# Edge attributes of a graph network kept in full precision, in bands of 32 partitions

## The chip, the cores and the metric

The kernel runs on one core of a Trainium2 chip as one launch. The time is that of one execution on the device in microseconds (us), and lower is better. The engines are TensorE (PE; its weight loads are listed as PEld), VectorE (DVE), ScalarE (ACT), GpSimd (POOL) and SyncE (SP). Each engine takes its instructions in the order in which they are written, and they meet over semaphores.

## The reference

A stack of graph networks and feed-forward layers over 1875 nodes of 256 features. Its first stage, the one that the change bears on, is a network of four layers over 31875 edges, which are ordered by their destination. Each edge has 32 attributes.

```python
def _gine(x, src, dst, edge_attr, W1, b1, W2, b2, eW, eb, eps):
    e = edge_attr @ eW + eb      # 31875 x 32 by 32 x 256
    m = jax.nn.relu(x[src] + e)
    agg = jax.ops.segment_sum(m, dst, num_segments=N)
    h = (1.0 + eps) * x + agg
    return jax.nn.relu(h @ W1 + b1) @ W2 + b2

h = _gine(x, src, dst, edge_attr, W1[0], b1[0], W2[0], b2[0], eW[0], eb[0], eps[0])
for k in range(1, 4):
    y = jax.nn.relu(_layernorm(h, gamma[k], beta[k]))
    h = h + _gine(y, src, dst, edge_attr, W1[k], b1[k], W2[k], b2[k], eW[k], eb[k], eps[k])
```

Behind it come a feed-forward layer with a capacity, an attention over edges with eight relations (it uses the same sorted edges), mixtures of experts and two graph convolutions. The change leaves them as they are.

## The kernel before, in words

**Order of the program.** `sort_edges` brings the edges into 264 chunks of 128 (`EC`), so that each chunk's edges go to nodes of one tile of 128 (15 tiles). It ends in `unpack_rows`. Then `pair_edges` builds tables for a later stage, mostly with GpSimd, and `gine_stack` runs the four layers: a layer norm, `gine_edges` (the edge loop) and `gine_mlp` (two products by 256 x 256 weights). All stages run one behind the other.

**Unpacking.** The 264 chunks arrive as rows of 36 words in 11 groups of `K` = 24 chunks. SyncE issues the loads of 9 chunks of each group, ScalarE those of 7, GpSimd those of 8 (`lanes`, L360). When a group is there, VectorE writes its 32 attributes four times side by side in bf16 (L440 and `split3`, L322 to L332): the high part, the middle part (what is left behind the high part), the low part, and the high part again. TensorE turns each chunk, 128 edges by 4 x 32 parts, with a bf16 transpose (L408, 264 of them, four to a PSUM bank), and ScalarE (22) and VectorE (44) copy the banks to `g.attrs_t` (L368), one block of 128 partitions by 128 edges for each chunk. VectorE takes out sources, destinations, types and weights too: for ten groups at once behind the tenth group's split, and for the last group behind its own (L417 to L427). `g.attrs_t` is a bf16 view of `g.edge_space`, 128 x 16896 words, whose memory the later attention uses again.

**Edge loop.** `gine_edges` runs once in each layer, over 264 chunks:

- GpSimd fetches for each chunk the 128 rows of the sources, 256 words each, from the table in DRAM with one indirect DMA (L833). The ring `got` has `RING` = 24 places. Before it issues chunk c it waits until the sum product of chunk c - 24 is done.
- TensorE makes the edge product of chunk c, two bf16 products over 128 rows that add up in one PSUM bank (L883, L884): the four parts of the attributes by parts of the weights, so that the sum stands for the full-precision product. Before it, it waits until VectorE has added chunk c - 4 (`summed`), which frees the bank.
- VectorE adds the edge product to the gathered rows (L922) once both are there. It also makes the one-hot matrices of the destinations, four chunks at a time (L844).
- ScalarE applies the relu in place (L901).
- TensorE makes the sum product of chunk c - 3 right behind the edge product of chunk c: gathered rows by one-hot matrix, two halves of 128 x 128 in full precision (L893). They wait for the relu (`msg_ready`) and for the bank that VectorE empties (`added`).
- VectorE adds the sum product of chunk c - `LAG` (4) to the accumulator `stack_acc` (L930).

The weights of the edge product, 32 x 256, are loaded four times below each other into `ew` (L869). VectorE splits them like the attributes and arranges `w_a` and `w_b` (L904 to L913), and TensorE waits for that at the start of each layer (`split`).

```python
pe.wait_ge(summed, c - 3)
nc.tensor.matmul(p_edge[c % 4][:, 0:D], g.attrs_t[:, c, :], w_a[:, :], start=True, stop=False)
nc.tensor.matmul(p_edge[c % 4][:, 0:D], g.attrs_t[:, c, :], w_b[:, :], start=False, stop=True).then_inc(edge_done, 1)
```

Of the kernel before, what the change touches and what calls it, by code (L numbers as in the profile page):

```python
# [8 lines left out]
BF16 = mybir.dt.bfloat16  # L9
# [325 lines left out]
def unpack_rows(nc, g, ph, valid, sorted_rows=None, chunks=None, first_i=None):  # L335
# [3 lines left out]
    NG, Q = EC // K, K // 4  # L339
    assert K * NG == EC and Q * 4 == K  # L340
    rows = ph.sb("rows", [P, EC, ROW])
    left = ph.sb("left", [P, 2, K, ED])
    parts = ph.sb("parts", [P, 3, K, 4, ED], BF16)
    local_i, local = ph.sb("local_i", [P, EC], I32), ph.sb("local", [P, EC])
    p_turned = [ph.ps(f"p_turned{b}", [P, 4, P], BF16) for b in range(8)]
    loaded, split, turned = ph.sem("loaded"), ph.sem("split"), ph.sem("turned")
    moved = [[ph.sem(f"moved{n}_{k}") for k in range(NG)] for n in range(3)] if chunks is not None else None
    stored = [ph.sem("stored_a"), ph.sem("stored_v")]
    lanes = [slice(0, 9), slice(9, 16), slice(16, K)]
    by_act = [n for n in range(NG * Q) if n % 3 == 0]  # L350
    by_dve = [n for n in range(NG * Q) if n % 3]
# [10 lines left out]
    def registers_of(eng, n):  # L362
        return [eng.alloc_register(f"{ph.name}_first{n}_{u}") for u in range(lanes[n].stop - lanes[n].start)]

    def store(eng, copy, who, mine, n):

        eng.wait_ge(turned, n + 1)
        copy(g.attrs_t[:, 4 * n:4 * n + 4, :], p_turned[n % 8][:, :, :]).then_inc(stored[who], 1)  # L368

    @block.sync  # L370
    def _(sp):
        if chunks is None:
            sp.dma_start(rows[:, :, :], sorted_rows.rearrange("(p c) w -> p c w", p=P)).then_inc(loaded, 16)
        else:
            registers = registers_of(sp, 0)
            for k in range(NG):
                load(sp, 0, k, registers)

    @block.gpsimd
    def _(pool):  # L380
        if chunks is not None:
            registers = registers_of(pool, 2)
            for k in range(NG):
                load(pool, 2, k, registers)

    @block.scalar
    def _(act):
        registers = registers_of(act, 1) if chunks is not None else None
        lag = 2
        for k in range(NG + lag):  # L390
            if registers and k < NG:
                load(act, 1, k, registers)
            for n in by_act:
                if n // Q == k - lag:
                    store(act, nc.scalar.copy, 0, by_act, n)

    @block.tensor
    def _(pe):
        for n in range(NG * Q):
            if n % Q == 0:  # L400
                pe.wait_ge(split, n // Q + 1)
            if n >= 8:
                if (n - 8) % 3 == 0:
                    pe.wait_ge(stored[0], by_act.index(n - 8) + 1)
                else:
                    pe.wait_ge(stored[1], by_dve.index(n - 8) + 1)
            for k in range(4):
                ins = nc.tensor.transpose(p_turned[n % 8][:, k, :], parts[:, n // Q % 3, n % Q * 4 + k, :, :].rearrange("p a w -> p (a w)"),  # L408
                                          g.ident_b[:, :])
            ins.then_inc(turned, 1)  # L410

    @block.vector
    def _(v):

        def fields(some):

            nc.vector.tensor_copy(g.src[:, some], rows[:, some, C_SRC].bitcast(I32))  # L417
            nc.vector.tensor_scalar(local_i[:, some], rows[:, some, C_DST].bitcast(I32), P - 1, None, ALU.bitwise_and)
# [10 lines left out]
        if chunks is None:  # L429
            v.wait_ge(loaded, 16)  # L430
        for k in range(NG + 1):
            if k < NG:
                if chunks is not None:
                    for n in range(3):
                        v.wait_ge(moved[n][k], 16 * (lanes[n].stop - lanes[n].start))
                some = slice(k * K, (k + 1) * K)
                a = rows[:, some, 0:ED]
                if k >= 3:
                    v.wait_ge(turned, (k - 2) * Q)
                nc.vector.tensor_copy(parts[:, k % 3, :, 3, :], a)  # L440
                split3(nc, v, a, [parts[:, k % 3, :, j, :] for j in range(3)], left[:, k % 2, :, :])
                v.drain()
                v.sem_inc(split, 1)
            if k == NG - 2:
                fields(slice(0, k * K + K))
            if k == NG:
                fields(slice((NG - 1) * K, EC))
            for n in by_dve:
                if n // Q == k - 1:
                    store(v, nc.vector.tensor_copy, 1, by_dve, n)  # L450
# [397 lines left out]
def gine_edges(nc, g, table, edge_w, acc):  # L848
# [3 lines left out]
    with Phase(nc, "gine") as ph:  # L852
        ew, left = ph.sb("ew", [P, D]), ph.sb("left", [P, D])
        parts = ph.sb("parts", [P, 3, D], BF16)
        w_a, w_b = ph.sb("w_a", [P, D], BF16), ph.sb("w_b", [P, D], BF16)
# [4 lines left out]
        loaded, split = ph.sem("loaded"), ph.sem("split")  # L860
# [1572 lines left out]
def build(nc, i, out):  # L2433
    Phase.count, Phase.spent = 0, []
    with ExitStack() as stack:
# [57 lines left out]
```

## Time and profile before

| | |
|---|---|
| median of 3 runs | 4661.29 us (4660.78 to 4661.66) |
| the profiled execution's own time | 4685.71 us |
| its span in the profile | 4684.1 us |
| mean granted clock of TensorE over the span | 0.778 |
| busy: TensorE, its weight loads | 2923.7 us (62%), 2401.0 us (51%) |
| busy: VectorE, GpSimd, ScalarE | 2212.2 us (47%), 1871.3 us (40%), 867.9 us (19%) |
| gathers L833 | 1056, 1024.5 us, mean 970 ns |
| sum products L893 | 4224 records, 846.2 us, mean 334 ns |
| edge products L883, L884 | 338.3 us and 336.8 us, mean 320 and 319 ns |
| VectorE's additions L922, L930 | 440.2 us and 438.9 us, mean 418 ns |
| edge loops of the four layers, from the first gather's issue | 180 to 588, 653 to 1063, 1131 to 1540, 1606 to 2015 us |

Times of instructions are microseconds from the span's start. A bracket behind an instruction tells how long its engine had been idle before it and what ended the wait: "remote" is a semaphore that no engine's instruction raised (here a transfer that landed), "issue" means that nothing in the profile was waited for. A full-precision product has more than one record: one product of 128 x 128 has two.

### The profile page before, as it was taken

The numbers are of one execution on the slowest core, as the hardware profiler recorded it, in microseconds if no ns is written. First come the engines' busy times: TensorE is split into PE (matmuls) and PEld (weight loads), VectorE is DVE, ScalarE is ACT, GpSimd is POOL, SyncE is SP. The second block draws the span as 40 slices with busy tenths as digits, with TensorE's granted clock in tenths as the row PEclk, the third lists the DMA queues.
The fourth block names the chain that finished last, engine by engine and source line by source line (L and its number), as shares of the span: only waits on it lengthen the run. The fifth ranks groups of instructions, "written<-read, shape, count | busy, mean of one in ns | idle before, by whom it ended". The sixth has DMA issues, their size and how long they took to land. (4 is left out here: it accounts for less than half of the span.)

```text
span 4684.1 us, 57224 instructions
## 1 busy us (share of the span) xinstructions
PE 2923.7 (62%) x16851; PEld 2401.0 (51%) x16852; DVE 2212.2 (47%) x5663; ACT 867.9 (19%) x2228; POOL 1871.3 (40%) x1982
## 2 busy tenths in 40 slices
PE   3566746664666566642568626665949639947392
PEld 3455535553555355522556413335938639936382
DVE  6655645554555555564243437681064421134113
ACT  1122312221222122210112100001300103310020
POOL 4366546664666466624323467731010020020212
PEclk7788878777887778875678657676979859978696
DMA  6633323332333233303312133315947449945594
GB/s 157 217 89 89 78 65 89 88 83 59 89 90 88 57 87 89 89 15 124 100 55 74 28 82 93 92 41 190 304 145 240 150 159 328 325 150 174 181 333 128
DMA packets 357397, 598.97 MB, mean 128 GB/s; under 512 B 81862, under 2 KB 239864, under 8 KB 354808
## 3 DMA queue, kind: packets, MB, share of 16 engines
q1 hardware_dynamic: 245816, 357.76, 23.3%
q0 software_dynamic: 88640, 214.25, 16.3%
q10 hardware_dynamic: 22656, 23.54, 1.5%
q8 instruction: 132, 2.16, 0.2%
q14 instruction: 153, 1.25, 0.1%
HBM read 499.63 MB, written 95.75 MB: 127 GB/s over the span
## 5 line engine op out<-in xcount | busy, mean ns | idle before, releaser
L833 POOL DMA_INDIRECT gine_got<-gine_table,src x1056 | 1024.5, 970 | 619.7 <-issue 251.1
L893 PE MATMUL gine_p_sum<-gine_hot,gine_got 128*128 128x128 f32 x4224 | 846.2, 334 | 565.1 <-DVE stack_acc L930 200.1
L893 PEld LDWEIGHTS gine_p_sum<-gine_hot,gine_got 128*128 128x128 f32 x4224 | 707.4, 238 | 719.0 <-issue 648.6
L922 DVE TENSOR_TENSOR gine_got<-gine_got,gine_p_edge 128x256 f32<-128x256 f32 x1056 | 440.2, 418 | 633.5 <-PE gine_p_edge L884 365.0
L901 ACT ACTIVATE gine_got<-gine_got 128x256 f32<-128x256 f32 x1056 | 439.0, 417 | 1201.1 <-issue 750.5
L488 POOL DMA_INDIRECT adjacency<-value,place x264 | 281.1, 1065 | 475.9 <-POOLq L54 166.2
L930 DVE TENSOR_TENSOR stack_acc<-stack_acc,gine_p_sum 128x256 f32 x1056 | 438.9, 416 | 3.5 <-issue 0.7
L883 PE MATMUL gine_p_edge<-gine_w_a,edge_space 128*128 128x256 bf16 x1056 | 338.3, 320 | 42.6 <-issue 34.7
L1368 PE MATMUL ffn_p_h<-ffn_xt,ffn_w 128*128 128x128 f32 x2864 | 347.3, 279 | 1.1 <-DMA ffn_w<-in_L_ffn_w 0.7
L1368 PEld LDWEIGHTS ffn_p_h<-ffn_xt,ffn_w 128*128 128x128 f32 x2864 | 337.3, 196 | 3.8 <-DMA ffn_w<-in_L_ffn_w 2.6
L884 PE MATMUL gine_p_edge<-gine_w_b,edge_space 128*128 128x256 bf16 x1056 | 336.8, 319 | 0.0
L1380 PE MATMUL ffn_p_y<-ffn_w,ffn_ht 128*128 128x256 f32 x1432 | 328.8, 380 | 4.7 <-DMA ffn_w<-in_L_ffn_w 3.9
L2224 POOL DMA_INDIRECT edge_space<-h_table,hrow x264 | 273.8, 1037 | 123.0 <-issue 74.6
L2259 PE MATMUL inorder_p_sum<-edge_space,inorder_hot 128*128 128x265 f32 x528 | 230.9, 553 | 145.2 <-DVE edge_space L2332 95.9
L1434 DVE TENSOR_TENSOR ffn_y<-ffn_p_y,ffn_b 128x256 f32<-128x256 f32 x112 | 47.6, 425 | 549.4 <-PE ffn_p_y L1380 549.4
L1405 ACT ACTIVATE ffn_ht<-ffn_p_h,ffn_b 128x128 f32<-128x128 f32 x716 | 204.8, 368 | 548.3 <-PE ffn_p_h L1368 548.3
L1633 PE MATMUL gcn_p_out<-gcn_h,gcn_a 128*128 128x256 f32 x1350 | 298.7, 379 | 0.0
L1380 PEld LDWEIGHTS ffn_p_y<-ffn_w,ffn_ht 128*128 128x128 f32 x1432 | 263.6, 190 | 38.3 <-DMA ffn_w<-in_L_ffn_w 6.7
L1633 PEld LDWEIGHTS gcn_p_out<-gcn_h,gcn_a 128*128 128x128 f32 x1350 | 253.8, 190 | 32.9
L2259 PEld LDWEIGHTS inorder_p_sum<-edge_space,inorder_hot 128*128 128x128 f32 x528 | 110.8, 252 | 236.6 <-issue 230.0
L1146 POOL IOTA route_e_idx<- 128x8 f32 (+1 forms) x3 | 0.4, 135 | 570.2 <-POOLq L54 570.2
L844 DVE TENSOR_TENSOR gine_hot<-iota_free,dst 128x512 f32<-128x512 f32 x264 | 182.6, 692 | 66.1 <-PE gine_p_sum L893 33.0
(398 smaller groups left out, 3526.2 us busy)
## 6 DMA issues: line engine op xcount, KB each, us to landing
gcn_a<-adjacency SPq DMA_DIRECT2D x270, 320.0 KB
ffn_w<-in_L_ffn_W SPq DMA_DIRECT2D x74, 1024.0 KB
ffn_w<-in_L_ffn_w SPq DMA_DIRECT2D x60, 1024.0 KB
ffn_w<-in_L_ffn_w SPq DMA_DIRECT2D x90, 512.0 KB
adjacency<-zero_row ACTq DMA_DIRECT2D x3, 7200.0 KB, 43.8
gine_got<-gine_table,src POOLq DMA_INDIRECT x1056
h_table<-score_rows SPq DMA_DIRECT2D x15, 1056.0 KB
adjacency<-zero_row SPq DMA_DIRECT2D x1, 7200.0 KB, 28.1
```

Source lines behind the costliest of these rows:

```text
L488: pool.indirect_dma_start(self.tables[c % 2], bass.IndirectOffsetOnAxis(ap=self.place[:, c:c + 1], axis=0), self.value[:, c:c + 1], None). ...
L833: pool.indirect_dma_start(got[:, c % RING, :], None, table, bass.IndirectOffsetOnAxis(ap=rows[:, c:c + 1], axis=0)).then_inc(gathered[c % ...
L883: nc.tensor.matmul(p_edge[c % 4][:, 0:D], g.attrs_t[:, c, :], w_a[:, :], start=True, stop=False)
L884: nc.tensor.matmul(p_edge[c % 4][:, 0:D], g.attrs_t[:, c, :], w_b[:, :], start=False, stop=True).then_inc(edge_done, 1)
L893: ins = nc.tensor.matmul(p_sum[d % 4][:, half * P:(half + 1) * P], got[:, d % RING, half * P:(half + 1) * P], hot[:, d % HOTS, :], start=T ...
L901: nc.scalar.activation(got[:, c % RING, :], got[:, c % RING, :], ACT.Relu).then_inc(msg_ready, 1)
L922: nc.vector.tensor_tensor(got[:, c % RING, :], got[:, c % RING, :], p_edge[c % 4][:, 0:D], ALU.add).then_inc(summed, 1)
L930: nc.vector.tensor_tensor(a, a, p_sum[d % 4][:, 0:D], ALU.add).then_inc(added, 1)
L1368: ins = nc.tensor.matmul(p_h[n % 2][m // 4][:, m % 4, :], w1_sb[:, n % 2, k, m * P:(m + 1) * P], xt[:, n % 2, k, :], start=(k == 0), stop= ...
L1380: ins = nc.tensor.matmul(p_y[n % 2][:, 0:D], ht[:, n % 2, m, :], w2_sb[:, n % 2, m, :], start=(m == 0), stop=(m == m_all - 1))
L1633: ins = nc.tensor.matmul(p_out[d][:, 0:D], a[:, n % RA, d * P:(d + 1) * P], h[:, t, :], start=(t == 0), stop=(t == T - 1))
L2259: nc.tensor.matmul(p_sum[c % SUMS][:, 0:WIDE], hot[:, c % HOTS, :], got[:, c % HELD, :], start=True, stop=True).then_inc(agg_done, 1)
```

## The change

The attributes are no longer split. In unpacking VectorE makes one full-precision copy of a group (`packed`), so that four chunks by 32 attributes lie side by side, and TensorE turns four chunks at once with a full-precision transpose, 66 in all, three to each of two PSUM banks a group. VectorE alone stores them (two copies of 128 x 384 a group); ScalarE only issues loads. `g.attrs` then has chunk c in the band of partitions 32 (c mod 4) to 32 (c mod 4) + 31. In the edge loop one full-precision product over the 32 rows of that band takes the place of the two bf16 products over 128 rows; all four bands of `ew` hold the same weights already. The splitting of the weights at the start of each layer goes, and TensorE waits for their load.

```diff
@@ unpack_rows
-    parts = ph.sb("parts", [P, 3, K, 4, ED], BF16)
+    packed = ph.sb("packed", [P, 3, K, ED])
-    p_turned = [ph.ps(f"p_turned{b}", [P, 4, P], BF16) for b in range(8)]
+    p_turned = [ph.ps(f"p_turned{b}", [P, 4, P]) for b in range(8)]
...
         def _(pe):
-        for n in range(NG * Q):
+        for n in range(NG * B):
...
-            for k in range(4):
-                ins = nc.tensor.transpose(p_turned[n % 8][:, k, :], parts[:, n // Q % 3, n % Q * 4 + k, :, :].rearrange("p a w -> p (a w)"),
-                                          g.ident_b[:, :])
+            for k in range(S):
+                c = (n % B * S + k) * 4
+                ins = nc.tensor.transpose(p_turned[n % 8][:, k, :], packed[:, n // B % 3, c:c + 4, :].rearrange("p c w -> p (c w)"),
+                                          g.ident[:, :])
...
-                nc.vector.tensor_copy(parts[:, k % 3, :, 3, :], a)
-                split3(nc, v, a, [parts[:, k % 3, :, j, :] for j in range(3)], left[:, k % 2, :, :])
-                v.drain()
-                v.sem_inc(split, 1)
+                nc.vector.tensor_copy(packed[:, k % 3, :, :], rows[:, k * K:(k + 1) * K, 0:ED]).then_inc(packed_ready, 1)
...
-            for n in by_dve:
-                if n // Q == k - 1:
-                    store(v, nc.vector.tensor_copy, 1, by_dve, n)
+            for n in range((k - 1) * B, k * B):
+                if n >= 0:
+                    v.wait_ge(turned, n + 1)
+                    nc.vector.tensor_copy(g.attrs[:, n * S:(n + 1) * S, :], p_turned[n % 8][:, 0:S, :]).then_inc(stored, 1)
@@ gine_edges
-            pe.wait_ge(split, 1)
+            pe.wait_ge(loaded, 64)
...
-                    nc.tensor.matmul(p_edge[c % 4][:, 0:D], g.attrs_t[:, c, :], w_a[:, :], start=True, stop=False)
-                    nc.tensor.matmul(p_edge[c % 4][:, 0:D], g.attrs_t[:, c, :], w_b[:, :], start=False, stop=True).then_inc(edge_done, 1)
+                    band = slice(c % 4 * ED, (c % 4 + 1) * ED)
+                    nc.tensor.matmul(p_edge[c % 4][:, 0:D], g.attrs[band, c // 4, :], ew[band, :], start=True, stop=True).then_inc(edge_done, 1)
...
-            v.wait_ge(loaded, 64)
-            split3(nc, v, ew[:, :], [parts[:, k, :] for k in range(3)], left[:, :])
-            nc.vector.memset(w_b[:, :], 0.0)
-            v.drain()
-            for q, part in enumerate((0, 0, 0, 1)):
-                nc.vector.tensor_copy(w_a[q * ED:(q + 1) * ED, :], parts[q * ED:(q + 1) * ED, part, :])
-            for q, part in enumerate((2, 1)):
-                nc.vector.tensor_copy(w_b[q * ED:(q + 1) * ED, :], parts[q * ED:(q + 1) * ED, part, :])
-            v.drain()
-            v.sem_inc(split, 1)
@@ the program
+            g.attrs = g.edge_space[:, 0:EC // 4 * P].rearrange("p (n e) -> p n e", e=P)
```

TensorE's order where the edge loop of a layer begins, before (four edge products ahead, then the sum product of chunk 0):

```order
L883 MATMUL gine_p_edge<-gine_w_a,edge_space 128x256
L884 MATMUL gine_p_edge<-gine_w_b,edge_space 128x256
L893 MATMUL gine_p_sum<-gine_hot,gine_got 128x128 x2
L883 MATMUL gine_p_edge<-gine_w_a,edge_space 128x256
L884 MATMUL gine_p_edge<-gine_w_b,edge_space 128x256
L893 MATMUL gine_p_sum<-gine_hot,gine_got 128x128 x2
```

and now, at the same place:

```order
L863 MATMUL gine_p_edge<-gine_ew,edge_space 128x256 x4
L872 MATMUL gine_p_sum<-gine_hot,gine_got 128x128 x2
L863 MATMUL gine_p_edge<-gine_ew,edge_space 128x256
L872 MATMUL gine_p_sum<-gine_hot,gine_got 128x128 x2
L863 MATMUL gine_p_edge<-gine_ew,edge_space 128x256
```

The places in the order are the same; one product over 32 rows stands between every two pairs of sum products over 128 rows, where two products over 128 rows stood.

VectorE's order for the last group of unpacking, before (the first four L368 store the group before it, the last four the last group):

```order
L440 CAST unpack_parts<-unpack_rows 128x24x32
L326 CAST unpack_parts<-unpack_rows 128x24x32
L328 TENSOR_TENSOR unpack_left<-unpack_rows,unpack_parts 128x768
L330 CAST unpack_parts<-unpack_left 128x24x32
L332 TENSOR_TENSOR unpack_parts<-unpack_left,unpack_parts 128x24x32
L368 COPY edge_space<-unpack_p_turned 128x512 x4
L417 COPY src<-unpack_rows 128x24
L418 TENSOR_SCALAR unpack_local_i<-unpack_rows 128x24
L419 CAST etype<-unpack_rows 128x24
L420 COPY weight<-unpack_rows 128x24
L427 TENSOR_SCALAR dst<-dst 128x24
L368 COPY edge_space<-unpack_p_turned 128x512 x4
```

and now:

```order
L423 COPY unpack_packed<-unpack_rows 128x768
L431 COPY edge_space<-unpack_p_turned 128x384 x2
L406 COPY src<-unpack_rows 128x24
L407 TENSOR_SCALAR unpack_local_i<-unpack_rows 128x24
L408 CAST etype<-unpack_rows 128x24
L409 COPY weight<-unpack_rows 128x24
L416 TENSOR_SCALAR dst<-dst 128x24
L431 COPY edge_space<-unpack_p_turned 128x384 x2
```

Four of the five instructions ahead of the stores are gone, and of the stores two remain of every four; the small ones between them stay (three of them are not shown in either list).

## Rows read from the trace of the kernel before

**Rows 1.** timeline of the gathers (POOL), layer 0: columns: start us, us, engine, line, instruction, [idle before]
```profile
180.07 1.00 POOL L833 DMA_INDIRECT gine_got<-gine_table,src  x1 [74.27 <-POOLq L54]
...
252.51 0.94 POOL L833 DMA_INDIRECT gine_got<-gine_table,src  x1 [1.68 <-remote]
...
567.72 1.04 POOL L833 DMA_INDIRECT gine_got<-gine_table,src  x1 [0.30 <-issue]
```

**Rows 2.** timeline of VectorE at the same moment, layer 0
```profile
252.32 0.42 DVE L922 TENSOR_TENSOR gine_got<-gine_got,gine_p_edge 128x256 f32<-128x256 f32 x1 [0.72 <-remote]
```

**Rows 3.** the other gather loop (relational attention), L2224: durations ns min/median/max
```profile
L2224 POOL DMA_INDIRECT edge_space<-h_table,hrow x264: 940/946/1784, 2709.7 to 3092.9; - x132
```

**Rows 4.** windows, line L922 alone: us, VectorE busy (count), granted clock, DMA share
```profile
569.00:586.00 17.00, 8.42 (x20) 0.96 0.16 15
280.00:380.00 100.00, 28.47 (x68) 0.82 0.31 89
```

**Rows 5.** timeline of TensorE in layer 0
```profile
300.04 0.61 PE L893 MATMUL gine_p_sum<-gine_hot,gine_got 128*128 128x128 f32 x4
300.48 0.27 PE L883 MATMUL gine_p_edge<-gine_w_a,edge_space 128*128 128x256 bf16 x1
...
300.70 0.61 PE L893 MATMUL gine_p_sum<-gine_hot,gine_got 128*128 128x128 f32 x4
...
306.69 0.68 PE L893 MATMUL gine_p_sum<-gine_hot,gine_got 128*128 128x128 f32 x4 [1.97 <-DVE stack_acc L930]
307.21 0.27 PE L883 MATMUL gine_p_edge<-gine_w_a,edge_space 128*128 128x256 bf16 x1
...
309.57 1.06 PE L893 MATMUL gine_p_sum<-gine_hot,gine_got 128*128 128x128 f32 x4
...
310.85 0.68 PE L893 MATMUL gine_p_sum<-gine_hot,gine_got 128*128 128x128 f32 x4
```

**Rows 6.** timeline of VectorE, end of the edge loop, layer 0
```profile
579.34 0.69 DVE L844 TENSOR_TENSOR gine_hot<-iota_free,dst 128x512 f32<-128x512 f32 x1
...
582.58 0.70 DVE L844 TENSOR_TENSOR gine_hot<-iota_free,dst 128x512 f32<-128x512 f32 x1
```

**Rows 7.** timeline of SyncE's queue, unpacking
```profile
29.10 63.32 SPq L360 DMA_DIRECT2D unpack_rows<-in_edge_rows  x99
```

**Rows 8.** DMA issues: KB each, median us from issue to landing
```profile
unpack_rows<-in_edge_rows ACTq DMA_DIRECT2D x77, 18.0 KB, 2.2
```

**Rows 9.** timeline of VectorE, last group of unpacking
```profile
97.12 0.55 DVE L440 CAST unpack_parts<-unpack_rows 128x768 bf16<-128x768 f32 x1
...
100.96 1.42 DVE L368 COPY edge_space<-unpack_p_turned 128x512 bf16<-128x512 bf16 x4
...
103.50 1.41 DVE L368 COPY edge_space<-unpack_p_turned 128x512 bf16<-128x512 bf16 x4
```

**Rows 10.** timeline of VectorE, start of layer 0's edge loop
```profile
182.47 0.29 DVE L326 CAST gine_parts<-gine_ew 128x256 bf16<-128x256 f32 x1 [6.48 <-DMA gine_ew<-in_L_gnn_eW]
...
185.63 0.45 DVE L912 COPY gine_w_b<-gine_parts 32x256 bf16<-32x256 bf16 x2
```

**Rows 11.** timeline of TensorE, full-precision products of 256 columns
```profile
3274.46 3.62 PE L1380 MATMUL ffn_p_y<-ffn_w,ffn_ht 128*128 128x256 f32 x16
```

**Rows 12.** timeline of TensorE, relational attention, two windows of the order
```profile
3106.22 0.33 PE L2237 MATMUL inorder_p_carry<-inorder_upto,inorder_shift 96*96 96x1 f32 x2
3106.41 0.31 PE L2240 MATMUL inorder_p_carry<-inorder_upto,inorder_shift 88*96 88x1 f32 x2
...
3106.75 0.47 PE L2259 MATMUL inorder_p_sum<-edge_space,inorder_hot 128*128 128x265 f32 x1
...
3117.83 0.33 PE L2237 MATMUL inorder_p_carry<-inorder_upto,inorder_shift 96*96 96x1 f32 x2
3118.09 0.33 PE L2240 MATMUL inorder_p_carry<-inorder_upto,inorder_shift 64*96 64x1 f32 x2
...
3118.53 0.47 PE L2259 MATMUL inorder_p_sum<-edge_space,inorder_hot 128*128 128x265 f32 x1
```

More of the change, by code:

```diff
@@ L338, in unpack_rows @@
     K = 24
-    NG, Q = EC // K, K // 4
-    assert K * NG == EC and Q * 4 == K
+    NG, B = EC // K, 2
+    S = K // 4 // B
+    assert K * NG == EC and S * B * 4 == K
     rows = ph.sb("rows", [P, EC, ROW])
-    left = ph.sb("left", [P, 2, K, ED])
-    parts = ph.sb("parts", [P, 3, K, 4, ED], BF16)
+    packed = ph.sb("packed", [P, 3, K, ED])
     local_i, local = ph.sb("local_i", [P, EC], I32), ph.sb("local", [P, EC])
-    p_turned = [ph.ps(f"p_turned{b}", [P, 4, P], BF16) for b in range(8)]
-    loaded, split, turned = ph.sem("loaded"), ph.sem("split"), ph.sem("turned")
+    p_turned = [ph.ps(f"p_turned{b}", [P, 4, P]) for b in range(8)]
+    loaded, packed_ready, turned, stored = ph.sem("loaded"), ph.sem("packed_ready"), ph.sem("turned"), ph.sem("stored")
     moved = [[ph.sem(f"moved{n}_{k}") for k in range(NG)] for n in range(3)] if chunks is not None else None
-    stored = [ph.sem("stored_a"), ph.sem("stored_v")]
     lanes = [slice(0, 9), slice(9, 16), slice(16, K)]
-    by_act = [n for n in range(NG * Q) if n % 3 == 0]
-    by_dve = [n for n in range(NG * Q) if n % 3]
     block = ph.block()
@@ L360, in load, with loads, group_in @@
             eng.dma_start(rows[:, c, :], chunks[bass.ds(row0, P), :]).then_inc(moved[n][k], 16)
[L362 to L368, printed above, removed]
+    def loads(eng, n):
+        registers = [eng.alloc_register(f"{ph.name}_first{n}_{u}") for u in range(lanes[n].stop - lanes[n].start)]
+        for k in range(NG):
+            load(eng, n, k, registers)
+    def group_in(eng, k):
+        if chunks is None:
+            eng.wait_ge(loaded, 16)
+        else:
+            for n in range(3):
+                eng.wait_ge(moved[n][k], 16 * (lanes[n].stop - lanes[n].start))
     @block.sync
@@ L374, in _ @@
         else:
-            registers = registers_of(sp, 0)
-            for k in range(NG):
-                load(sp, 0, k, registers)
+            loads(sp, 0)
+    @block.scalar
+    def _(act):
+        if chunks is not None:
+            loads(act, 1)
     @block.gpsimd
@@ L381, in _ @@
         if chunks is not None:
[L382 to L395, printed above, removed]
+            loads(pool, 2)
     @block.tensor
     def _(pe):
-        for n in range(NG * Q):
-            if n % Q == 0:
-                pe.wait_ge(split, n // Q + 1)
+        for n in range(NG * B):
+            if n % B == 0:
+                pe.wait_ge(packed_ready, n // B + 1)
             if n >= 8:
[L403 to L406, printed above, removed]
-            for k in range(4):
-                ins = nc.tensor.transpose(p_turned[n % 8][:, k, :], parts[:, n // Q % 3, n % Q * 4 + k, :, :].rearrange("p a w -> p (a w)"),
-                                          g.ident_b[:, :])
+                pe.wait_ge(stored, n - 7)
+            for k in range(S):
+                c = (n % B * S + k) * 4
+                ins = nc.tensor.transpose(p_turned[n % 8][:, k, :], packed[:, n // B % 3, c:c + 4, :].rearrange("p c w -> p (c w)"),
+                                          g.ident[:, :])
             ins.then_inc(turned, 1)
@@ L427, in fields @@
             nc.vector.tensor_scalar(g.dst[:, some], g.dst[:, some], -1.0, None, ALU.add)
-        if chunks is None:
-            v.wait_ge(loaded, 16)
         for k in range(NG + 1):
             if k < NG:
[L433 to L437, printed above, removed]
-                if k >= 3:
-                    v.wait_ge(turned, (k - 2) * Q)
-                nc.vector.tensor_copy(parts[:, k % 3, :, 3, :], a)
-                split3(nc, v, a, [parts[:, k % 3, :, j, :] for j in range(3)], left[:, k % 2, :, :])
-                v.drain()
-                v.sem_inc(split, 1)
+                group_in(v, k)
+                if k >= 3:
+                    v.wait_ge(turned, (k - 2) * B)
+                nc.vector.tensor_copy(packed[:, k % 3, :, :], rows[:, k * K:(k + 1) * K, 0:ED]).then_inc(packed_ready, 1)
             if k == NG - 2:
@@ L852, in gine_edges @@
     with Phase(nc, "gine") as ph:
-        ew, left = ph.sb("ew", [P, D]), ph.sb("left", [P, D])
-        parts = ph.sb("parts", [P, 3, D], BF16)
-        w_a, w_b = ph.sb("w_a", [P, D], BF16), ph.sb("w_b", [P, D], BF16)
+        ew = ph.sb("ew", [P, D])
         got = ph.sb("got", [P, RING, D])
@@ L859, in gine_edges @@
         p_sum = [ph.ps(f"p_sum{b}", [P, 512]) for b in range(4)]
-        loaded, split = ph.sem("loaded"), ph.sem("split")
+        loaded = ph.sem("loaded")
         gathered = [ph.sem(f"gathered{u}") for u in range(RING)]
```

## The prediction

> **What bounds the kernel now.** I read the grouped rows of the page first, to see what the changed lines weigh, then the timelines of the edge loop engine by engine, to see which wait ends last, then the end of unpacking. The busy shares (TensorE 62%, VectorE 47%, GpSimd 40%) name no engine as the bound, and they are means over many stages.
>
> *Edge loop.* GpSimd issues a gather in 0.95 us and the next 0.30 us later, which is 1.25 us. From the first issue of layer 0 at 180.07 to the last at 567.72 it takes 1.474 us a chunk on average (263 steps) [rows 1]. The difference is the ring. At 252.32 VectorE has waited 0.72 us for something that no engine's instruction raised, a landed gather, and 0.19 us later GpSimd, idle for 1.68 us, issues again [rows 1, 2]. So a late landing stops VectorE and TensorE, which frees no place, and that stops GpSimd. The attention's gather loop, with a longer ring and other consumers, runs at (3092.9 - 2709.7) / 263 = 1.457 us [rows 3], so the pace comes from the gathers and not from who consumes them. TensorE needs less: the sum product takes 0.44 us (300.04 to 300.48) and the two edge products together 0.22 us (300.48 to 300.70), 0.66 us a chunk at the full clock, and 1.28 us, from the sum product at 309.57 to the next at 310.85, at the lower one [rows 5]. VectorE needs 3.24 / 4 = 0.81 us a chunk [rows 6]. In mid-loop the granted clock is 0.82 [rows 4], between the levels of 1.2 and 2.4 GHz.
>
> *The tail of each layer.* After the last issue VectorE still adds 20 chunks between 569 and 586 us at a clock of 0.96 [rows 4]. That is 0.85 us a chunk, about its own 0.81: here the gathers are behind it and VectorE is the bound. This is the one stretch of the loop in which a slower TensorE is paid at once.
>
> *Unpacking.* SyncE issues 99 loads in 63.32 us and ends at 92.42 [rows 7]. A load lands 2.2 us after its issue [rows 8], so the last group is there at about 94.6. VectorE takes it at 97.12 and ends at 103.50 + 1.41 = 104.91 [rows 9]: at the end of unpacking VectorE is late.
>
> **The change part by part.**
>
> *Unpacking: -6.3 us.* On the last group five instructions (97.12 to 100.96, 3.84 us) become one copy of 128x768, between 0.55 us (the cast of that size) and 0.96 us (what the subtractions take); I take 0.8. Four stores that take 1.42 us [rows 9] become two of 128x384 full precision. An addition of 256 columns with an operand in PSUM takes 0.42 [rows 2], which gives at most 0.6 each; I take 0.5. The small instructions stay: 100.96 + 1.34 = 102.30 to 103.50, 1.2 us. From 94.6 that gives 94.6 + 0.8 + 1.0 + 1.2 + 1.0 = 98.6, and 104.91 - 98.6 = 6.3. Everything behind it starts earlier. Bounds: 4 (the last load lands at 97) and 8 (the stores at bf16's 0.35). ScalarE's 22 stores were not on this path; moving them to VectorE costs two short copies a group where 5.8 us lie between groups. TensorE's six transposes of 128x128 cost about 0.22 us each by the sum products [rows 5], 1.3 us a group beside the small instructions: nothing, up to 0.5 us at the lower clock.
>
> *Start of each layer: 0.* The split runs from 182.47 to 186.08 [rows 10] and goes; TensorE can start 3.6 us earlier, in four layers 14.4 us. The gathers have been issuing since 180.07, and the loop follows their pace, not TensorE's start: VectorE has to catch up 3.6 us over 264 chunks and does so in a few. What covers it is that pace. If the ring stalled in the first chunks because of it, up to 14.4 us would come back.
>
> *Edge product.* One full-precision product of 256 columns takes 2 records of 3.62 / 16 = 0.226 us [rows 11], so 0.44 us where 0.22 stood. That makes a chunk 0.88 us at the full clock and 1.76 us at the lower one. A product over 32 rows is not cheaper by its rows: nothing in the rows shows a price that falls with them.
>
> *The change of rows.* Between every two sum products over 128 rows now stands a product over 32. The trace shows something like it in one place: a product over 96 rows followed by one over 88, then a 128-row one, from 3106.22 to 3106.75, 0.53 us; the same with 64 rows in the middle, from 3117.83 to 3118.53, 0.70 us [rows 12]. A pair of changes costs 0.17 us there. Moreover a weight load lies today beside the product ahead of it: the sum product takes 0.44 where it follows on another, and 0.52 from 306.69 to 307.21 where it comes out of a wait [rows 5]. With two loads a chunk no longer covered that is 0.17 + 2 x 0.08 = 0.33. So a chunk costs 0.88 (nothing for it), 1.05, or 1.21 us. I take 1.21, as both loads stand directly at a change of rows. The Trainium skill ("TensorEngine Tiling (Array Packing)", Key Properties) says that changing the tiling mode, and not only the tile, drains TensorE; it gives no price. Rows 12 agree, with 0.17 us a pair. By this page alone the edit costs more than nothing, which speaks against the change.
>
> In mid-loop 0.88 to 1.21 us lie under 1.474 and cost nothing, while the clock is full. In the tail TensorE takes VectorE's place as the bound: 20 chunks x (1.21 - 0.81) = 8 us, in four layers 32 us; at 1.05 it is 19 us, at 0.88 6 us.
>
> **The sum.** On the profiled execution, 4685.7 us: - 6.3 + 0 + 32 = + 26, or 4711. The median of the runs is 24.4 us below that execution (0.5%), so 4661.3 + 26 = **4687 us**.
>
> **The rivals.**
>
> *B, the change of rows costs nothing.* For it: TensorE's loads run ahead of its products, and rows 12 hold products of one column, whose price may not carry over to 256. Against it: the same rows. Then - 6.3 + 6 = 0: 4661 us, no change (0.2%, or 9.3 us, is about what a measurement of this kernel can tell from none).
>
> *C, the starts of the layers count.* The edge loop's first chunks wait for the split (6.48 us of VectorE's idle time end with the load of `ew` [rows 10]), and if the ring's stop in the first 24 chunks comes from there, 14.4 us are gained beside the unpacking, with B's price for the tail: - 6.3 - 14.4 + 6 = - 15, 4646 us. Against it: the first stop of GpSimd that I read follows a landing [rows 1].
>
> *D, TensorE at the lower clock becomes the bound of the whole loop.* The place is mid-loop, where the clock was 0.82 so that about a third of the time was at the lower level [rows 4]. At the lower clock a chunk takes 1.76 us, or 1.76 + 0.33 = 2.09 with the change of rows, and both are over 1.474: it decides as soon as the clock stays low for most of the loop. A layer's loop then takes 264 x 1.76 = 465 us and 3 for its start instead of 408, which is 4 x 60 = + 240 and 4895 us; with 2.09 it is 552 + 3, + 147 a layer, 5243 us. For it: the clock was down in a third of the loop with TensorE waiting for landings, and waits remain. Against it: TensorE has a third more to do for each landing, and it stood at 0.96 where it was never kept waiting long [rows 4]. In a page's words: the Trainium skill ("TensorE: Matmul & The Clock Gate", Part 3) has the gain from products over 32 rows come only from several that run beside each other, and their loads overlap only where row groups differ. Here a product over all rows stands between any two, so by that page there is no gain at all from the bands; the trace has no such pair to show it.
>
> **How the numbers follow.** The forecast's case (a chunk of 1.05 to 1.21 us or somewhat more, seen in the tails) has 0.52, B 0.22, C 0.07, D 0.19. The top of the range is the tails at the lower clock: 4 x 20 x (2.09 - 0.81) = + 102 with nothing gained in unpacking, 4765 us; beyond lies D, which is left out nearly whole. The bottom is C with the tails free and the least from unpacking: - 4 - 15, 4642 us. Faster by over 0.2% is C, 0.07. Within 0.2% is B and the low end of the forecast's case, 0.22 + 0.05 = 0.27. Slower by over 0.2% is the rest, 0.66.
>
> **What the profile after would show.** Unpacking ends at 98 to 99 us instead of 104.9 and the first gather goes out 6 us earlier: else the first term is wrong. The edge product has two records of about 0.22 us at the full clock, and from a sum product to the next in the tail there are 1.05 to 1.21 us: at 0.9, B holds. From the last gather's issue to the loop's end it takes about 24 us instead of 17 to 20, with VectorE's waits there ended by TensorE. First to last gather of a layer stays near 388 us: if it falls by 3 us, C was right; if it grows by 60 or more while the granted clock of the loop is under 0.7, D was. If the clock of the loop rises well above 0.82 and the time falls, then TensorE's lower clock was costing more than the gathers let me see, and the reading of the bound was wrong.

## The result and the profile after

The changed kernel takes 5527.1 us (median of 4 runs, 5525.5 to 5528.8) against 4661.0 us before (4 runs beside it). The ratio is 1.186, interval 1.184 to 1.188: slower by 866 us. The forecast was 4687 us, in a range from 4642 to 4765.

The page of the changed kernel: slices of the span with TensorE's busy share and granted clock in tenths, then groups of instructions (busy us, mean ns, idle time before them and what ended it).

```profile
PE   4799997999969999799990578456666882986393
...
PEclk9555555555555555555555778567678995998697
...
L814 POOL DMA_INDIRECT gine_got<-gine_table,src x1056 | 997.8, 945 | 1380.4 <-PE gine_p_sum L872 1211.6
...
L872 PE MATMUL gine_p_sum<-gine_hot,gine_got 128*128 128x128 f32 x4224 | 1285.9, 461 | 66.2 <-issue 31.1
L863 PE MATMUL gine_p_edge<-gine_ew,edge_space 32*128 32x256 f32 x2112 | 1271.0, 710 | 30.2 <-DMA gine_ew<-in_L_gnn_eW 30.2
L891 DVE TENSOR_TENSOR gine_got<-gine_got,gine_p_edge 128x256 f32<-128x256 f32 x1056 | 444.5, 421 | 1460.1 <-PE gine_p_edge L863 1372.3
```

The clock stands at 5 tenths, the lower level of 1.2 GHz, wherever an edge loop runs, and TensorE is busy for nine tenths or more of each slice that lies wholly in one. VectorE waits 1372.3 us for edge products, where it waited 365.0 before, and GpSimd 1211.6 us for sum products. Before, each of the 170 stops of GpSimd of over 0.4 us (behind the first 24 chunks of a layer) came 3.1 us or more after the sum product that frees the place; now 892 of 910 such stops end 0.27 us after it. The bound has moved from the gathers to TensorE in the whole loop: this is rival D.

TensorE's timeline in mid-loop, layer 0 of the changed kernel, which answers to [rows 5]:

```profile
299.65 1.22 PE L872 MATMUL gine_p_sum<-gine_hot,gine_got 128*128 128x128 f32 x4
300.81 1.22 PE L863 MATMUL gine_p_edge<-gine_ew,edge_space 32*128 32x256 f32 x2
301.95 1.22 PE L872 MATMUL gine_p_sum<-gine_hot,gine_got 128*128 128x128 f32 x4
```

A chunk takes 301.95 - 299.65 = 2.30 us: sum product 1.16, edge product 1.14. Windows of the loops in layers 0 and 3 (us; busy time and count of TensorE, its loads, VectorE, ScalarE, GpSimd; granted clock, DMA share, GB/s) show the same, as layers 1 and 2 do (0.50 over each whole loop). The third line is the tail of layer 0:

```profile
180.00:740.00 560.00, 544.45 (x1422) 337.34 (x1420) 215.78 (x533) 98.60 (x237) 240.17 (x255) 0.50 0.21 60
2242.00:2815.00 573.00, 553.20 (x1448) 342.63 (x1448) 219.82 (x543) 101.27 (x243) 249.11 (x264) 0.50 0.21 61
745.00:794.00 49.00, 48.34 (x132) 30.77 (x131) 19.25 (x49) 8.32 (x20) 0.00 (x0) 0.50 0.01 2
```

**Where the time went**, in the two profiled executions: the loops, from the first gather's issue to the last addition, take 623.5, 623.5, 623.0 and 623.6 us; before they took 408.1, 410.1, 408.7 and 409.0. That is + 857.7 us. The first gather goes out at 170.43 instead of 180.07, - 9.6. The stretches between the loops are 2.8 us longer together, and all behind the last loop 9.0 us shorter. The sum is, but for rounding, the + 841.8 of the spans, 5525.9 - 4684.1. From its first to its last gather a layer now takes 572 us instead of 388 to 390, the sign that the prediction gave for D, and from the last gather's issue to the end 51 us instead of 20 to 21.

The end of unpacking in the changed kernel, VectorE, then the queues of SyncE and ScalarE:

```profile
91.78 0.56 DVE L423 COPY unpack_packed<-unpack_rows 128x768 f32<-128x768 f32 x1 [1.30 <-DMA unpack_rows<-in_edge_rows]
92.26 1.01 DVE L431 COPY edge_space<-unpack_p_turned 128x384 f32<-128x384 f32 x2
...
94.39 1.01 DVE L431 COPY edge_space<-unpack_p_turned 128x384 f32<-128x384 f32 x2
```

```profile
29.07 61.29 SPq L357 DMA_DIRECT2D unpack_rows<-in_edge_rows  x99
```

```profile
30.42 56.48 ACTq L357 DMA_DIRECT2D unpack_rows<-in_edge_rows  x77
```

It ends at 95.40 instead of 104.91. VectorE now waits for the last load, as forecast, but that load is there at 91.78 and not at 94.6: SyncE ends its issues at 90.36, 2.1 us earlier than before [rows 7], and the load is there 1.4 us behind that, not 2.2.

### The profile page after: what moved, and what is told of

The parts are those of the page before. It is cut to its first block and busy times, and to the rows that moved or that the text cites. A ratio compares the mean times of both kernels' runs of the same rounds, so it can differ in the third digit from the quotient of the medians.

```text
span 5525.9 us, 56629 instructions
## 1 busy us (share of the span) xinstructions
PE 4283.9 (78%) x16653; PEld 3029.3 (55%) x16654; DVE 2218.7 (40%) x5553; ACT 855.3 (15%) x2205; POOL 1840.5 (33%) x1982
## 3 DMA queue, kind: packets, MB, share of 16 engines
q14 instruction: 152, 1.25, 0.1%
## 5 line engine op out<-in xcount | busy, mean ns | idle before, releaser
L814 POOL DMA_INDIRECT gine_got<-gine_table,src x1056 | 997.8, 945 | 1380.4 <-PE gine_p_sum L872 1211.6
L872 PEld LDWEIGHTS gine_p_sum<-gine_hot,gine_got 128*128 128x128 f32 x4224 | 978.7, 322 | 745.4 <-issue 694.0
L872 PE MATMUL gine_p_sum<-gine_hot,gine_got 128*128 128x128 f32 x4224 | 1285.9, 461 | 66.2 <-issue 31.1
L863 PE MATMUL gine_p_edge<-gine_ew,edge_space 32*128 32x256 f32 x2112 | 1271.0, 710 | 30.2 <-DMA gine_ew<-in_L_gnn_eW 30.2
L891 DVE TENSOR_TENSOR gine_got<-gine_got,gine_p_edge 128x256 f32<-128x256 f32 x1056 | 444.5, 421 | 1460.1 <-PE gine_p_edge L863 1372.3
L863 PEld LDWEIGHTS gine_p_edge<-gine_ew,edge_space 32*128 32x128 f32 x2112 | 519.4, 308 | 264.4 <-issue 232.6
L1329 PE MATMUL ffn_p_x<-ident,ffn_x 128*128 128x128 f32 x224 | 45.2, 285 | 260.2 <-DMA ffn_x<-cap_slots 82.6
```

Source lines behind the costliest of these rows:

```text
L814: pool.indirect_dma_start(got[:, c % RING, :], None, table, bass.IndirectOffsetOnAxis(ap=rows[:, c:c + 1], axis=0)).then_inc(gathered[c % ...
L863: nc.tensor.matmul(p_edge[c % 4][:, 0:D], g.attrs[band, c // 4, :], ew[band, :], start=True, stop=True).then_inc(edge_done, 1)
L872: ins = nc.tensor.matmul(p_sum[d % 4][:, half * P:(half + 1) * P], got[:, d % RING, half * P:(half + 1) * P], hot[:, d % HOTS, :], start=T ...
L891: nc.vector.tensor_tensor(got[:, c % RING, :], got[:, c % RING, :], p_edge[c % 4][:, 0:D], ALU.add).then_inc(summed, 1)
```

## The experiments

Each is an edit of the changed kernel unless it says otherwise, and was run beside the kernel before on the same chip. That kernel took 4684.1 us beside e1 to e4, 4687.3 beside e5 to e7 (one run), 4372.0 beside e8 (one run) and 4679.2 beside e9 and e10. e2, e3, e5 to e8 and e10 were run once. "A layer" is the time of its edge loop as above.

### e1: the edge product over 128 rows

```diff
-        ew = ph.sb("ew", [P, D])
+        ew = ph.sb("ew", [P, 4, D])
...
+            sp.wait_ge(zeroed, 1)
             for q in range(4):
-                sp.dma_start(ew[q * ED:(q + 1) * ED, :], edge_w).then_inc(loaded, 16)
+                sp.dma_start(ew[q * ED:(q + 1) * ED, q, :], edge_w).then_inc(loaded, 16)
...
-                    band = slice(c % 4 * ED, (c % 4 + 1) * ED)
-                    nc.tensor.matmul(p_edge[c % 4][:, 0:D], g.attrs[band, c // 4, :], ew[band, :], start=True, stop=True).then_inc(edge_done, 1)
+                    first = c % 4 * ED // 128 * 128
+                    band = slice(first, first + 128)
+                    nc.tensor.matmul(p_edge[c % 4][:, 0:D], g.attrs[band, c // 4, :], ew[band, c % 4, :], start=True, stop=True).then_inc(edge_done, 1)
...
+            nc.vector.memset(ew[:, :, :], 0.0).then_inc(zeroed, 1)
```

`first` is 0 for every chunk here, so the product runs over all 128 rows. Its weights are zero in the three bands of the other chunks.

> The change, but the edge product runs over all 128 rows: four copies of the weights, each with zeros outside its band of 32. Still one full-precision product a chunk, no split, no change of rows between products. Theory ROWS (the loss comes from products over 32 rows among products over 128, through the clock, the changes of rows, or both): the granted clock of the edge loops goes back to about 0.8 or more, a chunk takes TensorE 0.88 us at the full clock, the loops follow the gathers again (about 405 to 412 us a layer), and the time is 4645 to 4670 us. Rival PRECISION (full precision alone makes TensorE too slow and keeps the clock down): the clock stays at 0.5, a chunk takes 1.76 us, a layer about 468 us, time 4880 us or more.

Measured: 4678.8 us (10 runs) against 4684.1 (19 runs), ratio 0.9987, interval 0.9978 to 0.9997. A layer takes 408 to 409 us. TensorE at the full and at the lower clock, then the window of the loop in layer 0, in e1 and in the kernel before:

```profile
299.70 0.60 PE L865 MATMUL gine_p_edge<-gine_ew,edge_space 128*128 128x256 f32 x2
300.14 0.61 PE L874 MATMUL gine_p_sum<-gine_hot,gine_got 128*128 128x128 f32 x4
300.58 0.60 PE L865 MATMUL gine_p_edge<-gine_ew,edge_space 128*128 128x256 f32 x2
...
304.78 1.06 PE L865 MATMUL gine_p_edge<-gine_ew,edge_space 128*128 128x256 f32 x2
305.64 1.06 PE L874 MATMUL gine_p_sum<-gine_hot,gine_got 128*128 128x128 f32 x4
306.49 1.06 PE L865 MATMUL gine_p_edge<-gine_ew,edge_space 128*128 128x256 f32 x2
```

```profile
180.00:560.00 380.00, 263.83 (x1458) 211.19 (x1457) 207.47 (x542) 100.06 (x241) 246.39 (x257) 0.90 0.32 89
```

```profile
180.00:560.00 380.00, 235.81 (x1431) 194.17 (x1432) 207.24 (x543) 98.90 (x238) 250.55 (x258) 0.79 0.31 90
```

Full precision is cleared: 0.88 us a chunk at the full clock, 1.71 at the lower one, the clock at 0.85 to 0.90 over the four loops (0.79 to 0.81 before), and the loop follows the gathers. The whole 866 us hang on the 32 rows, and not on how many values are other than zero: three quarters of the weights are zero here. The rows also price the waits at the changes of rows: at the lower clock the edge product takes 1.14 in the changed kernel and 0.86 here, the sum product 1.16 and 0.85, together 0.59 us a chunk.

### e2: 64 rows, and e3: more work over 128 rows

e2 is e1 with 64 in place of 128, so that the product runs over the 64 rows that hold the band. e3 is the change with this ahead of each edge product:

```diff
+                    nc.tensor.matmul(p_edge[c % 4][:, D:2 * D], g.attrs[:, c // 4, :], ew[:, :], start=True, stop=True)
```

> As e1, but the product runs over the 64 rows that hold the chunk's band (weights zero in the other half). The changes of rows stay, two a chunk; the product uses twice the rows of the change. Theory CHANGES (the changes of rows alone hold TensorE at the lower clock): as in the change, clock 0.50 in the loops, 2.2 to 2.3 us a chunk, about 5500 us. Theory SHARE (what counts for the clock is how many rows the products use): clock above 0.5 in parts of the loops or throughout, chunk near 1.2 us where it is full, time clearly below 5400 us.

> The change with more work: ahead of each 32-row edge product one full-precision product over 128 rows and 256 columns whose result nobody reads. Theory SHARE: the clock rises to near 1.0 in the loops, a chunk takes 0.44 + 0.44 + 0.44 + 0.14 to 0.33 = 1.5 to 1.65 us, and the kernel gets faster by doing more: 4700 to 4850 us. Theory CHANGES (as many changes of rows as in the change): clock stays 0.50, a chunk takes 2.3 + 0.88 = 3.2 us, a layer 840 us, time about 6470 us.

Measured: e2 5537.7 us, clock 0.50 in the loops, a layer 624.4 us, so nearly as the change (623.5). e3 6424.8 us, 843 us a layer, clock 0.50:

```profile
302.26 1.06 PE L862 MATMUL gine_p_edge<-gine_ew,edge_space 128*128 128x256 f32 x2
303.26 1.22 PE L864 MATMUL gine_p_edge<-gine_ew,edge_space 32*128 32x256 f32 x2
304.40 1.22 PE L873 MATMUL gine_p_sum<-gine_hot,gine_got 128*128 128x128 f32 x4
305.42 1.06 PE L862 MATMUL gine_p_edge<-gine_ew,edge_space 128*128 128x256 f32 x2
```

A chunk takes 3.16 us, 2.58 us of work at the lower clock and 0.58 at the two changes. Both came out as theory CHANGES had it, and as SHARE as I had worded it did not.

### e4: TensorE's order in groups of four, and e5: in pairs

```diff
-            for c in range(EC + 3):
-                if c < EC:
+            for b in range(EC // 4 + 1):
+                for c in range(4 * b, min(4 * b + 4, EC)):
...
-                if c >= 3:
-                    d = c - 3
+                for d in range(4 * b - 4, 4 * b):
+                    if d < 0:
+                        continue
```

(e5: the same in twos; the sum products of chunks 2b - 4 and 2b - 3 stand behind the edge products of 2b and 2b + 1.)

> The change with TensorE's order regrouped: the 32-row edge products of four chunks (four different bands) behind each other, then the sum products of the four chunks before. A pair of changes of rows for four chunks instead of one. Theory CHANGES: the extra 0.28 us at a half-speed product falls to a quarter, the clock is granted again, loops near the gathers' pace, time 4650 to 4720 us. Theory SHARE: the clock stays at 0.5 in most of the loop; a chunk takes 1.76 us + 0.14 = 1.9 us if the bands run one behind the other (about 5100 us), or 1.2 us if products in different bands run beside each other, which is under the gathers' pace, and then the time is 4650 to 4750 us in spite of the clock. Which of these holds is read from the granted clock and from the starts of the four products.

> The change with TensorE's order in pairs: two 32-row edge products, then the sum products of two chunks. One pair of changes of rows for two chunks (the change has one for each, e4 one for four, which brought the loops back to about 408 us). Waits at the changes: 0.59 us a pair at the lower clock in the change, so 0.30 us a chunk here. If the loss grows with the number of changes: clock between 0.5 and 0.76, a chunk of 2.0 us where the clock is low and 1.1 us where it is full, layers between 410 and 530 us, time 4700 to 5150 us. If the loss has a threshold and one pair for two chunks is over it: clock 0.50 throughout and 264 x 2.0 = 530 us a layer, about 5170 us.

Measured: e4 4688.0 us (10 runs), ratio 1.001, interval 1.000 to 1.002; a layer 410 to 413 us. e5 4806.1 us, a layer 442 us. TensorE in e4 (the first line at the full clock), then in e5, then both loops' windows:

```profile
786.45 1.34 PE L862 MATMUL gine_p_edge<-gine_ew,edge_space 32*128 32x256 f32 x8
787.72 2.05 PE L871 MATMUL gine_p_sum<-gine_hot,gine_got 128*128 128x128 f32 x16
```

```profile
301.28 1.22 PE L862 MATMUL gine_p_edge<-gine_ew,edge_space 32*128 32x256 f32 x4
302.44 2.08 PE L871 MATMUL gine_p_sum<-gine_hot,gine_got 128*128 128x128 f32 x8
304.44 1.22 PE L862 MATMUL gine_p_edge<-gine_ew,edge_space 32*128 32x256 f32 x4
```

```profile
180.00:560.00 380.00, 311.19 (x1446) 230.71 (x1447) 207.01 (x537) 99.88 (x240) 251.02 (x256) 0.72 0.32 89
```

```profile
180.00:580.00 400.00, 380.20 (x1436) 274.01 (x1435) 223.77 (x540) 100.24 (x240) 257.55 (x256) 0.50 0.30 85
```

Products in different bands run beside each other. In e5 two edge products take 1.16 us, from 301.28 to 302.44, with the waits at the changes in it; in the changed kernel one alone takes 1.14. In e4 four take 1.27 us at the full clock, where e1 needs 4 x 0.44. e5 has half the changes, and its clock is as low as the changed kernel's. A chunk takes 3.16 / 2 = 1.58 us, 0.72 less than 2.30: half of the waits at the changes would be 0.30 of that, and the rest, about 0.4, comes from the bands side by side. Both of my cases for e5 had the two run one behind the other. The Trainium skill ("TensorE: Matmul & The Clock Gate", Part 3) has products in different row groups overlap; the trace agrees, with these 1.16 us. The changed kernel, with a 128-row product between any two from the fifth chunk on, cannot use it.

### e6: everything over 32 rows, and e8: in one band

```diff
-                        ins = nc.tensor.matmul(p_sum[d % 4][:, half * P:(half + 1) * P], got[:, d % RING, half * P:(half + 1) * P],
-                                               hot[:, d % HOTS, :], start=True, stop=True)
+                        ins = nc.tensor.matmul(p_sum[d % 4][:, half * P:(half + 1) * P], got[0:ED, d % RING, half * P:(half + 1) * P],
+                                               hot[0:ED, d % HOTS, :], start=True, stop=True)
```

Both leave 96 of a chunk's 128 edges out of the sums. e8 has the line `band = slice(0, ED)` as well.

> The change, but the sum products run over 32 rows too (the first 32 edges of each chunk only, so 96 of 128 edges are left out of the sums). No product in the edge loops changes the number of rows, and all of them use few. Theory CHANGES (the interruptions at a change of rows keep the clock down): no waits at changes, clock back to 0.8 or more as in e1, chunk 0.88 us at the full clock, time 4640 to 4680 us. Theory SHARE (products over few rows do not bring the clock up, whatever stands between them): clock 0.50 in the loops though TensorE is as busy as in e1; a chunk takes 1.76 us, or less where neighbouring products in different bands run beside each other; a layer 408 to 470 us, time 4680 to 4900 us. The granted clock decides between them, the time may not.

> As e6 (every product of the edge loop over 32 rows, 96 of 128 edges left out of the sums), but all in the same band, rows 0 to 31: the edge product takes that band's attributes for every chunk, so its values are those of other edges. No change of rows, and no two bands beside each other: TensorE has 1.76 us to do for a chunk at the lower clock, without a gap, more than the gathers' 1.47, so it is never idle. Theory CHANGES (waits at the changes keep the clock down): the clock rises as in e1, loops at the gathers' pace, about 4680 us. Theory SHARE (few rows alone keep it down): 0.50 throughout the loops, 1.76 us a chunk, 465 to 468 us a layer, time about 4900 us.

Measured: e6 4676.5 us, 411 to 413 us a layer. e8 4767.0 us, 454 to 455 us a layer; that its time is not the 4900 of SHARE comes from 0.85 us a product where I had 0.88, and from the stages behind the last loop, which took 2578.1 us on its chip and 2659.1 in e6. The windows of layer 0's loop, e6 and then e8, and TensorE in e8:

```profile
180.00:560.00 380.00, 292.60 (x1437) 246.23 (x1437) 206.58 (x540) 99.97 (x240) 245.83 (x255) 0.50 0.32 89
```

```profile
200.00:560.00 360.00, 360.00 (x1268) 319.93 (x1267) 190.04 (x474) 87.79 (x212) 217.77 (x225) 0.50 0.29 83
```

```profile
301.40 1.06 PE L872 MATMUL gine_p_sum<-gine_hot,gine_got 32*128 32x128 f32 x4
302.25 1.06 PE L863 MATMUL gine_p_edge<-gine_ew,edge_space 32*128 32x256 f32 x2
303.10 1.06 PE L872 MATMUL gine_p_sum<-gine_hot,gine_got 32*128 32x128 f32 x4
```

e8 decides against CHANGES as the only cause. There is no change of rows and no wait, each product takes what it takes in e1 at the lower clock (0.85 us), TensorE is busy for 360.00 of 360 us, and the clock stays at 0.50. e1, with the same count of products and often idle, got 0.90. It is not the chip's doing: the kernel before had a mean clock of 0.833 over its span there. So products over few rows alone are enough for the low clock. In e6 the clock is as low, but there bands run side by side and the loop follows the gathers anyway.

### e7: the changes stay, most work over 128 rows

e2 with three unread 128-row products a chunk ahead of the edge product.

> e2 (64-row edge product, as many changes of rows as the change) with three more full-precision products over 128 rows a chunk whose results nobody reads. TensorE's work a chunk is 4.3 us at the lower clock, most of it over 128 rows, and the waits at the two changes 0.59 us are an eighth of it instead of a quarter. Theory SHARE (in the form that counts rows, waits included): the clock rises, a chunk takes 5 x 0.44 + 0.39 = 2.6 us, a layer about 690 us, time about 5800 us. If two changes a chunk keep the clock down whatever stands between them: 0.50, a chunk 4.9 us, a layer 1290 us, time about 8200 us.

Measured: 5833.1 us, 698 us a layer.

```profile
299.77 1.46 PE L865 MATMUL gine_p_edge<-gine_ew,edge_space 128*128 128x256 f32 x6
301.16 0.70 PE L867 MATMUL gine_p_edge<-gine_ew,edge_space 64*128 64x256 f32 x2
301.79 0.71 PE L876 MATMUL gine_p_sum<-gine_hot,gine_got 128*128 128x128 f32 x4
302.34 1.46 PE L865 MATMUL gine_p_edge<-gine_ew,edge_space 128*128 128x256 f32 x6
```

```profile
200.00:800.00 600.00, 599.25 (x2791) 419.82 (x2792) 213.46 (x528) 97.47 (x235) 235.10 (x235) 0.99 0.18 52
```

As many changes of rows as in the changed kernel, and the clock is at 0.99: the changes do not forbid it. With e8, a change is neither needed for the low clock nor enough for it by itself, which is what SHARE says. How work over few rows and over all rows weigh against each other is not shown: in e3 one 128-row product more left the clock at 0.50. e7 also gives the price of the two changes at the full clock, with 64 rows: 302.34 - 299.77 = 2.57 us a chunk, less 5 x 0.44, is 0.37 us.

### e9 and e10: what e1 is worth

> The kernel of e1 once more, to learn what it is worth and whether that depends on the chip (beside e8 the kernel before took 4372 us instead of 4661 to 4687). Where the kernel before takes about 4680 us: ratio 0.998 to 0.9995, since only the 9.6 us of unpacking are gained. On a chip where it takes about 4370 us the gathers land sooner, so that TensorE's 0.88 us (1.71 us at the lower clock) instead of 0.66 (1.28) may show in mid-loop: ratio 1.00 to 1.02 there. If only unpacking counts on such a chip as well: 0.998.

> The kernel before, unchanged, for its trace on the same chip. Where it takes about 4680 us: loops of 408 to 410 us, 1.474 us from gather to gather. Where it takes about 4370 us: loops shorter by some 75 us each, with VectorE no longer waiting for landings; then the pace of 1.474 us belongs to the chip and not to the kernel.

Measured: e9 4673.3 us (11 runs) against 4679.2 (15 runs), ratio 0.9986, interval 0.9977 to 0.9995. e10 4675.4 us. This chip was one of the usual kind, so what e1 does where the kernel before takes 4372 us was not seen.

## Why the prediction was wrong

- **The bound before: right, but not by way of the ring.** e1 makes TensorE's chunk 0.88 us instead of 0.66 and the loops stay at 408 to 409 us. "The difference is the ring" misread the stop at 252.51: that gather is chunk 50's, and the sum product of chunk 26, which frees its place, was over by 247. None of the 170 stops in the kernel before was the ring's. What held GpSimd was no engine's work ("remote" in the profile, so a landing as I read it), and the pace was the gathers' even so.
- **Unpacking, - 6.3: right way, 9.6 measured.** The copy and two stores took 0.56 and 1.01 us, near what I took. The rest is mostly the landing: I kept before's issue times [rows 7] and so let the last load land at 94.6; it was there at 91.8. ScalarE now issues its 77 loads in one go until 86.90. That its stores had held its loads back, and theirs SyncE's, was not tried apart.
- **Start of the layers, 0: right.** In e1 the splitting is gone too and TensorE starts 3.8 us behind the first gather (171.27 to 175.06) instead of 6.1 (180.07 to 186.16), and a layer takes as long as before. Rival C is out.
- **Full-precision product, 0.44 us: right** (e1), and free in mid-loop as I had it.
- **The tails, + 8 us a layer: right bound, wrong size.** TensorE sets them, as forecast, but at 2.30 us a chunk: 51 us instead of 20 to 21, in four layers + 122 us where I had + 32. The other 736 of the loops' 857.7 us lie between the first and the last gather, where I had nothing.
- **Price of the changes of rows, 0.33: about right at the full clock** (0.37 in e7, with 64 rows), and too low at the lower one, where I used the same 0.33 and it is 0.59. The 1-column products of [rows 12] gave 0.17 of it.
- **The step that failed** is "In mid-loop 0.88 to 1.21 us lie under 1.474 and cost nothing, while the clock is full", with the case against D that TensorE "has a third more to do for each landing". I held that more busy time would lift the clock or at least leave it. With products over all rows it did: 264 of 380 us busy and 0.90 in e1, 236 and 0.79 before. With the 32-row products the clock was 0.50 in all four loops, with TensorE busy in 544 of 560 us in layer 0, and a chunk became 1.71 + 0.59 = 2.30 us, 0.83 over the gathers' pace; 264 of them are 607 us, and with the start of the loop 623. D had 2.09 us in its worse form and 5243 us; with 0.59 in place of 0.33 it would have had + 0.26 x 264 x 4 = 275 more, 5518 us. The mechanism stood among the rivals, at 0.19; the range left it out.
- **Of the 214 us a layer** the lower clock without any wait at changes gives 454 - 408 = 46 (e8), and the waits at changes 0.59 x 264 = 156. The other 12 come, as I read it, from TensorE's waits at the loop's start, 15.6 us in layer 0 with 12.30 of them up to 208.01. They end with relus of gathered rows that VectorE had waited 13.13 us for, with the edge product long done. The kernel before waits there too (12.37 us up to 218.55), hidden in the gathers' pace; e8, on its chip, does not. The lower clock is what makes the waits count: at the full clock the same chunk would be, as an estimate from e1 and e7, 0.88 + 0.37 = 1.25 us, under the gathers' 1.474.
- **Open:** how much of the low clock in the changed kernel is the 32 rows and how much the waits at the changes. e8 shows that few rows suffice where nothing else runs; the changed kernel has full-row sum products too. A kernel with such waits and only full rows was not made, since the waits come with the change.

## What to carry to other kernels

Before narrowing a product's rows, ask what it does to the granted clock and not only how long the product takes: in e8 TensorE was busy without a gap and still ran at 1.2 GHz, and its products differed from e1's only in using few rows. If attributes must lie in bands, either fill the other rows with zeros in the moving operand, which cost nothing here (e1 and e9, 0.13% and 0.14% faster than before), or put products of different bands behind each other, so that they run side by side and the rows change seldom (e4, as fast as before). And a rival that sits one clock level away from the forecast belongs in the range, not beside it.

## What was not expected of the hardware

- Four full-precision products in four different bands take 1.24 us at the start of layer 0 in the changed kernel, and 3.78 us in e1, both with the clock at 0.50. The changed kernel, then e1:

```profile
173.64 1.24 PE L863 MATMUL gine_p_edge<-gine_ew,edge_space 32*128 32x256 f32 x8 [5.53 <-DMA gine_ew<-in_L_gnn_eW]
```

```profile
175.06 3.78 PE L865 MATMUL gine_p_edge<-gine_ew,edge_space 128*128 128x256 f32 x8 [6.34 <-DMA gine_ew<-in_L_gnn_eW]
```

- A change of rows costs on both sides of it: 0.28 us at a 32-row product and 0.31 at the sum product behind it, at the lower clock, and it is the same for 64 rows (e2). Part of it stands before the second record: the two records of an edge product start 0.59 us apart in the changed kernel and 0.43 in e1.
- The chip that ran e8 took 4372.0 us for the kernel before (one run), 6% less than the others, and in e8's trace gathers cost less too. The attention's gather loop is the same code in all these kernels. Its 264 gathers take 1.347 us each there, and 1.452 in e6, on another chip; in the other traces of this case it is 1.438 to 1.457. At the start of layer 0 VectorE waits in e6 for landings, 11.13 us in the longest of the waits. In e8 it waits 0.7 us in 1056 additions. e8, then e6, then the wait in e6:

```profile
L2193 POOL DMA_INDIRECT edge_space<-h_table,hrow x264: 942/946/1772, 2843.4 to 3197.7; - x132
```

```profile
L2193 POOL DMA_INDIRECT edge_space<-h_table,hrow x264: 943/949/1569, 2708.0 to 3089.9; - x132
```

```profile
207.41 0.42 DVE L891 TENSOR_TENSOR gine_got<-gine_got,gine_p_edge 128x256 f32<-128x256 f32 x1 [11.13 <-remote]
```

So the pace of gathers can differ from chip to chip. What the edge loop's 1.474 us would be on that chip is not shown: in mid-loop e8 is held by TensorE, at 1.58 us a gather, which is slower than 1.474.
